# Router logits of a fused attention and mixture-of-experts kernel taken from x Wr and from Wo Wr instead of from the swapped normed rows; another seam between the stages, another table, places and end

## The reference, cut to what matters

```
x1  = x + attention(layernorm(x), ctx, ctx) @ Wo + bo      # 16 heads of 16
n   = layernorm(x1)
p   = softmax(n @ Wr)                                      # 8 experts
w   = softmax(top_2(p)) at the two chosen experts, 0 elsewhere
out = x1 + sum_e w_e * ((silu(n @ G_e) * (n @ U_e)) @ D_e) # F = 512
```

## Time and profile before

| what | before |
|---|---|
| median of 3 runs | 1259.24 us (1256.96 to 1259.7) |
| profiled execution: its own time | 1258.72 us |
| its span, granted clock | 1256.9 us, 0.992 |
| PE busy | 1217.9 us (97%), 11246 matmul records |
| PEld busy | 995.8 us (79%) |
| DVE, ACT, POOL busy | 646.4, 561.7, 424.6 us |
| DMA | 112.45 MB, mean 89 GB/s |

### The profile page before, as it was taken

How to read it: one execution, slowest core, us unless ns; L and a number is a source line. 1 busy time by engine, 2 the same in 40 slices (tenths; PEclk the granted TensorE clock), 3 DMA queues, 4 the chain that set the end, 5 groups by cost and what they waited for, 6 DMA issues and landing times.

```text
span 1256.9 us, 30804 instructions
## 1 busy us (share of the span) xinstructions
PE 1217.9 (97%) x11246; PEld 995.8 (79%) x11247; DVE 646.4 (51%) x1762; ACT 561.7 (45%) x926; POOL 424.6 (34%) x354
## 2 busy tenths in 40 slices
PE   7999999999999999799999999999999999999995
PEld 5677776777767766588888888888888888888994
DVE  3778878888888878833473222222333322222331
ACT  4566666666666665435422222222222222223441
POOL 4112333333333333243455422222222223333322
PEclk9999999999999999899999999999999999999998
DMA  5444444544555432324444433333343333333432
GB/s 151 131 124 124 148 143 147 153 152 151 153 151 153 120 116 86 90 65 73 77 77 77 76 51 51 51 51 51 52 51 52 52 51 53 51 51 39 57 52 26
DMA packets 171586, 112.45 MB, mean 89 GB/s; under 512 B 103344, under 2 KB 158640, under 8 KB 171472
## 3 DMA queue, kind: packets, MB, share of 16 engines
q1 hardware_dynamic: 143984, 72.75, 23.8%
q0 software_dynamic: 26400, 37.09, 17.1%
q10 hardware_dynamic: 1088, 1.05, 0.2%
HBM read 48.59 MB, written 45.46 MB: 75 GB/s over the span
## 4 chain that ended last, share of the span: by engine, by line
PE 90%; DVE 4%; DMA 2%; issue 1%; ACT 1%; SPq 0%; POOL 0%; POOLq 0%; DVEq 0%
PE banks L539 72%; PE banks L568 5%; PE banks L582 5%; PE banks L593 4%; DVE row_max L1076 1%; PE banks L574 1%; PE banks L545 1%; DMA heads<-qT 1%; PE banks L609 1%; PE banks L617 1%; DVE q_less L1083 1%; DVE att_rows L1089 1%; DMA out<-x_sb,token 1%; PE banks L718 0%; SPq L291 0%
## 5 line engine op out<-in xcount | busy, mean ns | idle before, releaser
L487 POOL DMA_INDIRECT out<-x_sb,token x135 | 210.5, 1559 | 419.9 <-DVE x_sb L1398 377.8
L907 ACT ACTIVATE qT<-banks 128x1024 f32<-128x1024 f32 (+1 forms) x75 | 70.4, 938 | 464.4 <-PE banks L539 445.8
L1392 DVE TENSOR_TENSOR heads<-qT,banks 128x1024 f32<-128x1024 f32 (+1 forms) x75 | 83.6, 1114 | 349.1 <-PE banks L539 338.4
L539 PE MATMUL banks<-down_sb,heads 128*128 x1080 | 245.5, 379 | 0.9 <-DVE x_sb L1398 0.9
L539 PE MATMUL banks<-xnT,kT 128*128 128x256 f32 (+1 forms) x1216 | 242.8, 357 | 1.5 <-ACT probs L901 1.5
L539 PE MATMUL banks<-xnT,probs 128*128 128x256 f32 (+1 forms) x1184 | 238.7, 359 | 0.0
L539 PEld LDWEIGHTS banks<-xnT,kT 128*128 128x128 f32 x1216 | 211.8, 190 | 27.0 <-issue 1.9
L539 PEld LDWEIGHTS banks<-xnT,probs 128*128 128x128 f32 x1184 | 208.3, 190 | 25.2 <-issue 0.2
L539 PEld LDWEIGHTS banks<-down_sb,heads 128*128 128x128 f32 x1080 | 204.0, 190 | 28.3 <-issue 1.3
L440 POOL DMA_INDIRECT sorted_x<-xn,slots_now x128 | 125.3, 979 | 286.2 <-PE banks L568 143.1
L1076 DVE TENSOR_REDUCE row_max<-banks 128x16 f32<-128x2048 f32 x64 | 146.6, 2291 | 60.7 <-PE banks L568 60.6
(11 more groups left out here) (168 smaller groups left out, 1296.2 us busy)
## 6 DMA issues: line engine op xcount, KB each, us to landing
xn<-sorted_x SPq DMA_DIRECT2D x240, 64.0 KB
x_sb<-in_x SPq DMA_DIRECT2D x16, 512.0 KB, 3.9
ctxT_sb<-in_ctx SPq DMA_DIRECT2D x16, 512.0 KB
heads<-kT SPq DMA_DIRECT2D x128, 64.0 KB
heads<-qT SPq DMA_DIRECT2D x128, 64.0 KB
out<-x SPq DMA_DIRECT2D x16, 512.0 KB
gate_sb<-_L_ffn_kernel_gating_EDF SPq DMA_DIRECT2D x8, 512.0 KB
up_sb<-in_L_ffn_kernel_up_EDF SPq DMA_DIRECT2D x8, 512.0 KB
```

The source lines that it names most:

```text
L487: pool.indirect_dma_start(out=out[:, :], out_offset=bass.IndirectOffsetOnAxis(ap=token[:, v, h:h + 1], axis=0), in_=ys[:, 2 * u + h, :], i ...
L539: last = nc.tensor.matmul(dst, lhsT, rhs, start=(i == 0), stop=(i == len(pairs) - 1))
L907: nc.scalar.activation(gatedT[:, 0:w * F], gate_up[:, 0:w * F], ACT.Silu).then_inc(s_silu, 1)
L1392: nc.vector.tensor_tensor(fusedT[:, u, 0:w * F], gatedT[:, 0:w * F], gate_up[:, 1024:1024 + w * F], ALU.mult).then_inc(s_fuse, 1)
```

## The change

The router's logits are linear in x1, and x1 = x + bias + att @ Wo. So logits = rstd * (x1 @ Wr) - rstd * mean * (column sums of Wr), and x1 @ Wr = (x + bias) @ Wr + att @ (Wo Wr). Wo gets nine more columns (Wo Wr for eight experts, and one that keeps the row sum of x1 right); x @ Wr comes by `route_logits` from a transposed copy of x, a new input in DRAM that SP loads for each group (512 KB). The normed rows are no longer swapped; `second_norm` stays, as its rows go to `sorted_x`. Cut to what counts:

```diff
+WIDE = D + EXPERTS + 1
-        x_bo = sb("x_bo", [P, 2, GROUP, D])
+        x_bo = sb("x_bo", [P, 2, GROUP, WIDE])
 # SP: Wr in one transfer, and a column of bo; after the first spreads, ahead of load_x(1):
+            sp.dma_start(woT_sb, woT.rearrange("(c p) n -> p c n", p=P)).then_inc(s_woT, 16)
+            load_xT(0)
             sp.wait_ge(s_norm, 1)
 # SP, quarter 2, ahead of load_x(g + 2):
+                    if b == 2 and g + 1 < GROUPS:
+                        load_xT(g + 1)
 # SP, last line (POOL's own last wait for the same goes):
+            sp.wait_ge(s_acc, added(UNITS))
 # POOL: a mask up_to[8, 8] once; keep_x is as it was, into x_bo[:, u, :, 0:D]
 # PE
-                product(bank[:, 0:D], [(attnT[:, c * P:(c + 1) * P], wo_sb[:, c, :]) for c in range(DC)]).then_inc(s_proj, 1)
-            def x1_swapped(g, c, bank):
...
+                product(bank[:, 0:WIDE], [(attnT[:, c * P:(c + 1) * P], wo_sb[:, c, :]) for c in range(DC)]).then_inc(s_proj, 1)
 # wo_through_router: 4 products of 9 columns in quarter 0 of group 0;
 # router_constants: 6 products of 9 columns in quarter 1 of group 0, behind swap_max(1)
             def places(g, bank):
-                for b in range(GROUP):
-                    last = product(bank[:, b * EXPERTS:(b + 1) * EXPERTS],
-                                   [(before[:], chosen[:, b, :]), (ones[:], seen[:])]
-                                   + [(ones[:], chosen[:, a, :]) for a in range(b)])
+                nc.tensor.matmul(to, before[:], chosen[:], start=True, stop=False)
+                for a in range(GROUP - 1):
+                    nc.tensor.matmul(to[:, a + 1:GROUP], ones[:], chosen[:, a:a + 1, :].broadcast_to([P, GROUP - 1 - a, EXPERTS]),
+                                     start=False, stop=False)
+                last = nc.tensor.matmul(to, ones[:], seen[:].unsqueeze(1).broadcast_to([P, GROUP, EXPERTS]), start=False, stop=True)
 # PE, stage_a: swap_logits(g) and route_logits(g) for the group itself, not for g - 2
-                    if b >= 2 and prev:
-                        wait(pe, s_less, i * 2 + 2)
-                        x1_swapped(g - 1, b - 2, other_bank(i, 3))
 # PE, seam: the first gate product goes to banks 4 and 5
-            pe.wait_ge(s_n2Tc, (GROUPS - 1) * 2)
-            wait(pe, s_exp, SEQS * 3 - 1)
-            gate(0, 0, 2)
+            wait(pe, s_x1, SEQS - 2)
+            gate(0, 0, 2, 2)
 # PE, end (before: gate, up, down of the unit before, for the last unit too)
+            gate(UNITS - 1, (UNITS - 1) % 2, 1)
+            down_(UNITS - 2, UNITS % 2, 1)
+            up_(UNITS - 1, (UNITS - 1) % 2, 1)
             down_(UNITS - 1, (UNITS - 1) % 2, 1)
 # ACT: copy_x1T (two copies of 128x512 a group) goes
 # DVE
+            def keep_x_logits(g, u, bank):
+                wait(dve, s_logit, g + 1)
+                nc.vector.tensor_tensor(x_bo[:, u, :, D:WIDE], ..., bias_logits..., ALU.add).then_inc(s_x_logits, 1)
+            def keep_raw(g):
+                wait(dve, s_x1, g * GROUP + GROUP)
+                wait(dve, s_route, (g - 1) * ROUTE_STEPS + 1)
+                nc.vector.tensor_copy(raw[:], x1[:, :, D:D + EXPERTS]).then_inc(s_raw, 1)
-            def route_shift(g, bank):
-                steps.then(nc.vector.reduce_max(best[:], raw, AX.X))
-                steps.done(nc.vector.tensor_tensor(logits[:], raw, over_experts(best[:]), ALU.subtract))
+            def route_shift(g):
+                steps.done(nc.vector.tensor_tensor(logits[:], raw[:], over_experts(rstd2[:]), ALU.mult))
+                steps.then(nc.vector.tensor_tensor(tied[:], over_group(router_sums), over_experts(shift2[:]), ALU.mult))
+                steps.then(nc.vector.tensor_tensor(logits[:], logits[:], tied[:], ALU.add))
+                steps.then(nc.vector.reduce_max(best[:], logits[:], AX.X))
+                steps.done(nc.vector.tensor_tensor(logits[:], logits[:], over_experts(best[:]), ALU.subtract))
-            def add_up_tiles(steps, experts):
...
+            def add_up_tiles(steps, room):
+                steps.then(nc.vector.tensor_tensor(part, n_pairs..., up_to[:], ALU.mult))
+                steps.then(nc.vector.reduce_sum(tiles_to[:], part, AX.X))
 # DVE, stage_a, after take_max_off(i):
+                    if b == 1 and core:
+                        keep_x_logits(g, u, other_bank(i, 3)[:, P:2 * P])
                     if b == 1 and prev2:
-                        route_shift(g - 2, other_bank(i, 3)[:, P:2 * P])
+                        route_shift(g - 2)
 # add_residual of quarter 2 moves from behind turn_attn to right behind turn_att;
 # after route_first(g - 2), the last work of quarter 1:
+                    if b == 1 and prev:
+                        keep_raw(g - 1)
```

More of the change, by code:

```diff
@@ L646, in stage_a @@
                     wait(pe, s_turn, i - 1)
[L647 to L650, removed]
+                    if b == 1 and core:
+                        wait(pe, s_logitTc, g + 1)
+                    if i == 1:
+                        pe.wait_ge(s_wo_wide, 1)
+                    if b == 2 and core:
+                        wait(pe, s_x_logits, g + 1)
                     if b == 3 and prev2:
@@ L733, in _ @@
             pe.wait_ge(s_bv_rep, 1)
-            product(work[:, 0, 0:D], [(bv_rep[:, c, :], wo_sb[:, c, :]) for c in range(DC)]).then_inc(s_bvo, 1)
+            product(work[:, 0, 0:D], [(bv_rep[:, c, :], wo_sb[:, c, 0:D]) for c in range(DC)]).then_inc(s_bvo, 1)
             pe.wait_ge(s_piece_c, 2)
@@ L745, in expert_of, with up_or_gate @@
                 return pe.value_load(expert_table[0:1, bass.ds(t, 1)], min_val=0, max_val=EXPERTS - 1)
-            def up_or_gate(u, w, k, signal):
+            def up_or_gate(u, w, k, signal, place=None):
                 n = w * P
                 for f in range(FC):
-                    last = product(gate_up[:, 1024 * k + f * n:1024 * k + (f + 1) * n],
+                    at = 1024 * (k if place is None else place) + f * n
+                    last = product(banks[:, at // 512, at % 512:at % 512 + n],
                                    [(held[u][:, k * HALF + c * F + f * P:k * HALF + c * F + (f + 1) * P],
@@ L753, in up_or_gate, with gate @@
                 last.then_inc(signal, 1)
-            def gate(n, u, w):
+            def gate(n, u, w, place=0):
                 pe.wait_ge(s_xtc, n + 1)
@@ L758, in gate @@
                 wait(pe, s_silu, n)
[L759 removed]
+                up_or_gate(u, w, 0, s_gate, place)
             def up_(n, u, w):
@@ L779, in behind_tile @@
                 if t == 0:
-                    project(last - 1, work[:, 1, :])
+                    project(last - 1, banks[:, 7])
                 if t == 1:
@@ L1187, in tile_starts_passed @@
                                                    edges[:].unsqueeze(1).broadcast_to([P, EXPERTS, m]), ALU.is_gt))
-            def add_up_tiles(steps, experts):
-                if experts[0] == 1:
-                    steps.then(nc.vector.tensor_copy(tiles_to[:], n_pairs[:]))
-                for e in experts:
-                    steps.then(nc.vector.tensor_tensor(tiles_to[:, e:e + 1], tiles_to[:, e - 1:e], n_pairs[:, e:e + 1], ALU.add))
+            def add_up_tiles(steps, room):
+                part = room[:, 0:EXPERTS * EXPERTS].rearrange("p (a b) -> p a b", b=EXPERTS)
+                steps.then(nc.vector.tensor_tensor(part, n_pairs[:].unsqueeze(1).broadcast_to([P, EXPERTS, EXPERTS]), up_to[:],
+                                                   ALU.mult))
+                steps.then(nc.vector.reduce_sum(tiles_to[:], part, AX.X))
             def experts_of_tiles(steps, past, n):
@@ L1353, in stage_a @@
                         add_residual(i - 2, 0, u, other_bank(i, 0))
+                    if b == 2 and prev2:
+                        route_read_places(g - 2, other_bank(i, 2))
+                    if one:
+                        divide_by_sums(i - 1)
+                        turn_attn(i - 1)
+                    if b == 0 and prev3:
+                        route_rows(g - 3)
                     if i == 0:
@@ L1408, in behind_tile @@
                 if t == 1:
-                    add_residual(SEQS - 2, 2, 1, work[:, 1, :])
+                    add_residual(SEQS - 2, 2, 1, banks[:, 7])
                 if t == 2:
@@ L1412, in behind_tile @@
                 if t == 3:
+                    route_shift(GROUPS - 2)
+                    keep_raw(GROUPS - 1)
                     second_eps(GROUPS - 1)
-                if t == 5:
-                    route_shift(GROUPS - 2, att)
                 if t == 6:
```

240 lines of the change are left out of this document (125 added, 115 removed).

## The result

| | before | after |
|---|---|---|
| median | 1258.1 us (4 runs, 1256.29 to 1259.7) | 1278.7 us (4 runs, 1277.72 to 1280.77) |
| ratio | | 1.0166 [1.0146, 1.0187] |
| profiled: own time, span | 1258.72, 1256.9 us | 1280.77, 1279.0 us |
| granted clock of the span | 0.992 | 0.986 |

The forecast was 1278.0. The increase is 20.6 us by the medians and 22.1 us between the two profiled executions, where +18.6 was forecast. Part 1 of the page after, against the earlier trace rows: PE is busy for 10 us less, at 94% of the span instead of 97%, DVE for 36 us more.

The account below looks back on a forecast made before the run. PE was taken as the bound, with DVE hardly any slack in quarter 2; groups +30, group 10 -2.3, start +2.7, seam -6.4, experts -2.8, end -2.6 sum to +18.6: 1278 us median, range 1246 to 1297.

Parts of the forecast that it names:

- The hold: Quarter 2, groups 2 to 14: POOL's x_bo blocks a DVE operation on SBUF until it ends; PE waits 2.6 us.
- the meeting: Quarter 2: DVE, made 0.74 us later, issues an SBUF operation behind x_bo's start; before, seen in group 10 only.
- the start's terms: Start: loads issued ahead of x(1), their bytes, and six small products of router_constants; together +2.7 us, bounds 0 and +5.
- the chain to the scores: Quarter 3: ACT's copy, SP's issue and the transfer of spread queries before the next scores; 3.3 to 4.1 us.
- rest held: Quarter 2: DVE's rest, route_second's first operation, with two SBUF operands, held by x_bo until 291.53 instead of 288.66.
- Rival 3: Quarters 2 and 3: the hold, and PE's clock falls too; 1295 in half the groups, 1312 in all; chance 0.13.
- the 0.3 forecast: Quarter 3: of 0.5 us spared by a removed swap, 0.3 is kept, as scores wait for the spread queries.
- The seam: Between attention and expert stage: PE's waits, a clock fall and a swap go; -6.4 us, bounds -2 and -7.
- if the idle goes, the fall goes: Seam: without PE's 1.65 us wait for row_max the fall to 1.2 GHz goes too; -4.3 us in all.
- Expert stage and end: Expert stage: PE work removed, -2.8 us; end: earlier last down-but-one -0.6 and POOL's winding down -2.
- POOL's wait: End: POOL no longer waits for the landing before it winds down; -2 us, bounds 0 and -2.5.
- Case 2: Groups 2 to 14: DVE's extra steps are absorbed and PE keeps all it is spared; 1234 us, chance 0.12.

Follow-up runs that it names:

- E1: The changed kernel, with POOL's x_bo of quarter 2 also waiting for DVE's shift2; 1247.98 us, ratio 0.9918.
- e3: The kernel before, with three small DVE reduces added at the end of quarter 1's work in groups 2 to 15; 1285.57 us, ratio 1.0224.
- E6: The changed kernel, with keep_raw's copy written as a reduce over a dimension of one element; 1278.56 us, ratio 1.0158.
- e7: The kernel of e2, with x(1) loaded ahead of Wo^T and x^T(0), its statistics ahead of the copy of Wo Wr; 1237.74 us, single run.
- e2: The changed kernel, with DVE's route_shift moved from quarter 1 to the end of quarter 0; 1237.71 us, ratio 0.984.
- e8: The kernel of e2, with SP's load of x^T for the next group issued in quarter 1 instead of quarter 2; 1237.72 us, ratio 0.9874.
- e4: The kernel before, with its last wait (all adds landed) on SP instead of POOL; 1255.86 us, ratio 0.9986.
- e9: The kernel of e2, with x^T loaded for group 0 only, the other 15 groups' loads left out; 1237.56 us, ratio 0.9875.

## Why the prediction was right

**The hold is the cause, as forecast.** E1 takes only the meeting away and gains 31 us; e3 adds 0.3 us of DVE work to the kernel before, and with it the meeting, and loses 28. The price was read from one group of before (2.50 us from the scores' end to row_max, in the earlier trace rows) and carried over to 13. From the scores of sequence 8 to those of 59 this gave +27.7 us, and +29.5 came.

**That the total came so near is in part luck.** In the profiled executions the pieces add up to +22.1 us instead of +18.6: +1.8 in groups 2 to 14 and +2.5 at the seam are misses, and -0.2 and -0.5 in the last two stretches. By the medians it is +20.6. That 1278.7 is only 0.7 from 1278.0 comes of where the forecast started: a median of 1259.2 for the kernel before, which one more run lowered to 1258.1. Three sums in the prediction are off by a little: the start's terms add up to 2.8 at least and not 2.7, the chain to the scores to 3.2 to 4.0 us and not 3.3 to 4.1, and the chances of faster and slower come to 0.24 and 0.72. None changes the forecast.

**What is held was named wrongly.** The prediction booked keep_raw at 0.1 us and had rest held, with its two inputs in SBUF; by its own times keep_raw would start at 289.11, 0.03 us ahead of x_bo. It came 0.04 us behind x_bo, and it was held: a copy with one input is held too. The step behind it hardly changes, because the hold ends with x_bo whatever waits: row_max starts 3.20 us late where 3.10 was predicted, PE's wait was 2.57 instead of 2.6. E6 gives the case that was predicted, rest held for 2.24 us, at the same time of 1278.6. By the Trainium skill (SBUF — State Buffer, "Who interferes with whom") a copy can take the shared port pair as well, a reduce on this chip never does, and issue order alone decides who blocks; the copy (2.35 us), the reduce (0.19) and the 0.03 us of e7 agree with the three, where DVE is the one behind. The prediction had used only its sentence on two SBUF inputs.

**The clock's case came in part.** Rival 3 priced a fall at 2.6 us a group. In groups 3, 4, 8 and 14 quarter 2 took 11.3 to 11.5 us, at a granted clock of 0.85 or 0.86. In eight others it took 10.5 to 10.8 and in group 2 9.81, at 1.00. So a fall cost 0.8 to 1.0 us here and not 2.6, and it came in four of 13 groups. In group 8 the queries' product behind the wait took 3.29 us instead of the 1.88 of an undisturbed quarter. With those, the group's mean is 10.77 us where 10.5 was taken. PE's busy time is up by some 7 us in the whole stage, by e2; on the groups' period it is the 0.25 us above, about 3 in 13 groups, which the sum had at zero. Which groups fall is open: the idle time ahead of swap_max is about 2.6 us in all twelve from group 3 on, and in e6, where it is 2.5 in the same twelve, the clock fell in six (3, 4, 6, 7, 8, 13). Nor does it take the hold: in e1, e6 and e8 one quarter 0 each took 9.68 us instead of 8.06, at 0.82, behind a wait of 1.6 to 1.7 us for the queries, while in e2 a wait of 1.63 us was followed by no fall. Quarter 3 went from a mean of 8.02 us to 7.69, the 0.3 forecast.

**The seam was mis-sized: -3.9 instead of -6.4.** The wait that was to go did go: ahead of swap_max 0.31 us is left of 1.65. First a line of before, then after:

```profile
503.80 1.08 PE L617 MATMUL banks<-xn2T,wr_sb 128*32 128x128 f32 x16 [1.47 <-DVE att_rows L1089]
```

```profile
532.43 0.33 PE L597 MATMUL banks<-ident,row_max 128*128 128x128 f32 x1 [0.31 <-DVE row_max L1082]
534.23 0.94 PE L645 MATMUL banks<-xT_sb,wr_sb 128*32 128x128 f32 x16 [1.47 <-DVE att_rows L1095]
535.11 2.09 PE L605 MATMUL banks<-q_less,heads 32*128 32x128 f32 x32
...
554.52 0.19 PE L657 MATMUL banks<-chosen,before 128*128 128x32 bf16 x1 [1.94 <-DVE att_rows L1095]
...
562.77 2.42 PE L562 MATMUL banks<-xnT,kT 128*128 128x256 f32 x10
```

The step "if the idle goes, the fall goes" failed, as only the first of two idle times went. Right behind, PE waits 1.47 us for turn_att ahead of x Wr, exactly as it did in before ahead of the product with Wr, and the clock falls at 535 (scores_swapped 2.09 us instead of 1.17). It falls again at 545 (0.50 for 6 us, above) and at 554. The two stretches of the seam show the same: PE's idle time fell from 10.71 to 6.95 us, by 3.8, which is what the sum of -6.4 gives without its 2.6 for the clock, and its busy time from 35.32 to 35.15 only. That the gate product no longer waits for the exps was right: it stands with no wait at 562.77.

**The start was right by its sum, not by its parts.** It had x(1)'s later issue and bytes at 1.6 us, PE's new products in quarter 0 at nothing and router_constants at 1.2. Quarter 0 of group 0 went from 6.63 to 7.99 us, by PE's new products. Quarter 1 went from 8.56 to 9.84, and of these 1.28 us e7 gives 0.76 to x(1); that leaves 0.5 for router_constants, though they take 1.26 on PE, which in before waited 0.49 us there (ahead of the keys' product, for v_aug). So 0 and 1.6 stand for 1.4 and 0.8, and 1.2 for 0.5: the errors cancelled.

**Expert stage and end** came as worked out: -3.0 for -2.8, -3.1 for -2.6, of which e4 shows 2 us to be POOL's wait. That x^T's load is hidden holds within e9's 1.7 us. Case 2 (1234) is about what e2 gave once DVE was early enough.

## What to carry to other kernels

Before putting work on an engine that is "half idle", ask what it stands next to: in a quarter with 0.35 us of room, 0.74 us of added DVE work cost 2.6, since one of its instructions came just behind a long GpSimd instruction on SBUF (a copy by 0.04 us in group 8). Such a meeting is cheap to take away, by a wait that lets the long one start behind the short ones (31 us here) or by moving the short ones to where there is room (41 us). Here a single group in the trace of before that behaved unlike the others showed what twelve of them did once the order had shifted by that much.

## What the runs showed of the hardware

A copy of 128x32 fp32 from SBUF to SBUF that starts behind GpSimd's 128x1024 tensor_tensor lasts up to 2.39 us; a reduce of the same elements does not (0.19 us at most). Whether shift2 was held was decided by hundredths of a microsecond: 0.03 us behind x_bo it took 2.36 us, 0.02 ahead 0.16. POOL needs 6.6 to 6.8 us from its last issue to the end of the span even where it waits for nothing, and the landing of the last transfer fits beside that. In after the clock fell behind waits of 2.6 us in four groups and stayed at 1.00 behind the same wait in eight others; it fell behind 1.47 us at the seam. No run here tells what decides it.
